# A two-layer graph network: VectorE's transposed one-hot and its copies of x columns take a second operand from PSUM

## The reference

```
for each of two layers:
    z      = concat(x[dst], x[src], edge_attr)            # 320 per edge
    msg    = sigmoid(z @ Wf + bf) * softplus(z @ Ws + bs) # 128 per edge
    summed = segment_sum(msg, dst);  cnt = segment_sum(1, dst)
    out    = batchnorm(summed / max(cnt, 1)) + x
result = layernorm(x + out of layer 2)
```

## Time and profile before

| | |
|---|---|
| time, median of 3 runs | 2116.5 us (2115.28 to 2119.24) |
| span of the profiled execution | 2110.8 us |
| VectorE busy | 1801.2 us, 85% of the span |
| ScalarE busy | 1677.5 us, 79% |
| TensorE busy (weight loads) | 1557.2 us, 74% (1286.2 us, 61%) |
| GpSimd busy | 1515.1 us, 72% |
| mean granted TensorE clock | 0.925 of full speed |
| mean busy share of the DMA engines, most of the span | about 0.53 |

### The profile page before, as it was taken

One profiled execution on the slowest core, in us unless ns is written; L12 is line 12 of the kernel. 1 busy time (PEld: TensorE's weight loads), 2 busy tenths in 40 slices (PEclk: granted clock), 3 DMA queues, 4 the chain that ended last, 5 costly groups with the idle time before them and its releaser, 6 DMA issues. The chain is left out here.

```text
span 2110.8 us, 35689 instructions
## 1 busy us (share of the span) xinstructions
PE 1557.2 (74%) x8321; PEld 1286.2 (61%) x8321; DVE 1801.2 (85%) x4354; ACT 1677.5 (79%) x2908; POOL 1515.1 (72%) x1589
## 2 busy tenths in 40 slices
PE   7777767767767787677487777777676776877773
PEld 6666656656556666566376666666565665665652
DVE  6899989989889898898549999898898887988887
ACT  5798888878878788788467888888787887887884
POOL 6677777777777777777267777777777777777770
PEclk9999999999999899999799999999999998999995
DMA  8455555555555555555475555555555555555542
GB/s 291 138 156 166 156 166 155 163 158 156 158 160 156 155 156 165 152 157 155 147 224 156 154 166 165 156 163 156 156 158 161 155 155 156 162 157 156 154 143 62
DMA packets 161806, 336.71 MB, mean 160 GB/s; under 512 B 58866, under 2 KB 85610, under 8 KB 161671
## 3 DMA queue, kind: packets, MB, share of 16 engines
q0 software_dynamic: 74496, 202.13, 32.5%
q1 hardware_dynamic: 85654, 131.58, 20.4%
q10 hardware_dynamic: 1522, 1.72, 0.3%
HBM read 315.49 MB, written 19.81 MB: 159 GB/s over the span
## 5 line engine op out<-in xcount | busy, mean ns | idle before, releaser
L344 POOL DMA_INDIRECT pre<-s_rows,ends x1512 | 1451.3, 960 | 473.8 <-issue 448.1
L458 PE MATMUL pre_ps<-rhs,lhs 128*128 128x256 f32 x3136 | 854.8, 417 | 463.5 <-DVE lhs L696 462.1
L458 PEld LDWEIGHTS pre_ps<-rhs,lhs 128*128 128x128 f32 x3136 | 607.0, 204 | 676.1 <-DVE lhs L696 385.0
L716 DVE TENSOR_TENSOR pre<-pre_ps,pre 128x1024 f32<-128x1024 f32 x378 | 460.7, 1219 | 52.6 <-DMA pre<-s_rows,ends 51.1
L548 ACT ACTIVATE pre<-pre 128x512 f32<-128x512 f32 x392 | 246.9, 630 | 309.3 <-DVE pre L716 270.0
L471 PEld LDWEIGHTS sum_ps<-hot,msg 128*128 128x128 f32 x3136 | 441.6, 204 | 53.2 <-issue 15.5
L696 DVE TENSOR_SCALAR lhs<-lhs,base_f,part 64x256 f32<-64x256 int32 x784 | 340.9, 435 | 114.2 <-issue 106.5
L471 PE MATMUL sum_ps<-hot,msg 128*128 128x64 f32 x3136 | 418.1, 279 | 24.8 <-DVE sums L736 24.8
L553 ACT ACTIVATE logs<-pre 128x1024 f32<-128x1024 f32 x392 | 414.3, 1057 | 12.4
L543 ACT COPY rhs<-dst_ps 64x256 f32<-64x256 f32 x792 | 290.0, 366 | 24.8 <-PE dst_ps L445 6.6
L727 DVE TENSOR_TENSOR msg<-soft_ps,logs 128x512 f32<-128x512 f32 x392 | 271.0, 691 | 13.6
(11 more groups left out here) (88 smaller groups left out, 570.8 us busy)
## 6 DMA issues: line engine op xcount, KB each, us to landing
lhs<-dge_and_destination_cols SPq DMA_DIRECT2D x196, 512.0 KB
pre<-s_rows,ends POOLq DMA_INDIRECT x1512
s_rows<-logs SPq DMA_DIRECT2D x8, 512.0 KB, 7.1
s_rows<-x_t SPq DMA_DIRECT2D x7, 512.0 KB, 10.8
s_rows<-msg SPq DMA_DIRECT2D x6, 512.0 KB, 6.1
x_rows<-pre SPq DMA_DIRECT2D x12, 256.0 KB, 4.5
out<-y_out SPq DMA_DIRECT2D x12, 256.0 KB, 2.3
ends<-edge_ends SPq DMA_DIRECT2D x100, 16.0 KB, 3.6
```

The lines of the kernel that those rows point to most:

```text
L344: nc.gpsimd.indirect_dma_start(pre[:, slot(k, j), i, 0:width], None, rows, bass.IndirectOffsetOnAxis(ap=ends[:, k, j * TILES + i, 0:1], ax ...
L458: ins = nc.tensor.matmul(pre_ps[:, j % 2, i, :], lhs[:, j // 2, edges], rhs[:, j, i // 2, :], start=True, stop=not plain(b, k, j))
L716: nc.vector.tensor_tensor(rows, pre_ps[:, j % 2], rows, ALU.add).then_inc(s_pre[j], 1)
```

## The change

Two groups of columns of `sum_ps` that no matmul writes get fixed contents: `part_ps` holds the partition numbers, `ones_ps` a column of ones. They are filled once a layer. The transposed one-hot becomes a `scalar_tensor_tensor` whose second tensor is `part_ps`, read with a step of zero over the 256 columns. The copies of x columns become a product with `ones_ps`. Since PE writes the same bank, VectorE's wait for the window sums of step m - 4 (`s_sum`) moves to the start of the step, both copies stand between the two additions, and PE's first window sum waits for the copies of step 3.

```diff
+        part_ps, ones_ps = sum_ps[:, 0, 0, WIN:WIN + PAIRS], sum_ps[:, 0, 1, WIN:WIN + 1]
...
             def window_sum(g, j):
                 done(pe, s_msg, g, j, 0)
                 done(pe, s_hot, g, j, 0)
+                if isinstance(g, int) and g == 0 and j == 0:
+                    pe.wait_ge(s_cols[3], 2)
                 done(pe, s_added, g, j, 1)
...
                 after(nc.vector.tensor_tensor(flag[:, 1:2], flag[:, 0:1], sum_ps[0:1, 0, 0, 0:1], ALU.add))
+                v.wait_ge(iotas, 3)
+                after(nc.vector.tensor_copy(part_ps, t["part"][:]))
+                after(nc.vector.tensor_copy(ones_ps, t["ones"][:]))
...
             else:
                 v.sem_inc(planned, 1)
+                nc.vector.tensor_copy(part_ps, t["part"][:]).then_inc(scaled, 1)
+                nc.vector.tensor_copy(ones_ps, t["ones"][:]).then_inc(scaled, 1)
+                v.wait_ge(scaled, 2)
                 v.wait_ge(cnt_in, 16)
...
-                    v.wait_ge(scaled, c + 1)
+                    v.wait_ge(scaled, c + 3)
...
-                    ins = nc.vector.tensor_scalar(lhs[hot_rows[q], j // 2, at],
-                                                  lhs[hot_rows[q], j // 2, at].bitcast(I32),
-                                                  base_f[hot_rows[q], k, PAIRS * j + q:PAIRS * j + q + 1],
-                                                  t["part"][hot_rows[q], q:q + 1], ALU.subtract, ALU.is_equal)
+                    ins = nc.vector.scalar_tensor_tensor(lhs[hot_rows[q], j // 2, at],
+                                                         lhs[hot_rows[q], j // 2, at].bitcast(I32),
+                                                         base_f[hot_rows[q], k, PAIRS * j + q:PAIRS * j + q + 1],
+                                                         part_ps[hot_rows[q], q:q + 1].to_broadcast([WIN, PAIR]),
+                                                         ALU.subtract, ALU.is_equal)
...
             def add_up(g, j, q, at):
-                done(v, s_sum, g, j, 0)
...
+            def take_window(j, q, at):
+                return nc.vector.tensor_tensor(x_cols[:, j, q, :], x[:, bass.ds(at[PAIRS * j + q], WIN)],
+                                               ones_ps.to_broadcast([P, WIN]), ALU.mult)
...
-                ins = nc.vector.tensor_copy(x_cols[:, j, q, :], x[:, bass.ds(at[PAIRS * j + q], WIN)])
+                ins = take_window(j, q, at)
...
+                if four_back:
+                    done(v, s_sum, four_back[0], four_back[2], 0)
                 if live(0):
                     hot_transposed(b, k, j)
...
                     add_up(four_back[0], four_back[2], 0, sum_at)
                 if live(0):
                     window_cols(g, j, 0, cols_at)
+                    window_cols(g, j, 1, cols_at)
                 if four_back:
                     add_up(four_back[0], four_back[2], 1, sum_at)
-                if live(0):
-                    window_cols(g, j, 1, cols_at)
```

More of the change, by code:

```diff
@@ L833, in _ @@
                 for q in range(PAIRS):
-                    ins = nc.vector.tensor_copy(x_cols[:, j, q, :], x[:, bass.ds(cols_at[PAIRS * j + q], WIN)])
+                    ins = take_window(j, q, cols_at)
                 ins.then_inc(s_cols[j], 1)
```

## The result

The changed kernel takes 2124.22 us in the median of 20 runs (2116.0 to 2129.4), the kernel before 2116.35 us (2113.49 to 2119.38, 20 runs). The ratio is 1.0035, 95% interval 1.0028 to 1.0043: 7.9 us slower, where 2104.5 us had been forecast, 12.0 less than 2116.5. The profiled execution of the changed kernel took 2124.08 us with a span of 2122.3, so 1.8 us lie around the span, not the 5.7 that the prediction took; the profiled execution of before, with 1.8 us around its 2110.8, would be shorter than each of the 20 runs.

A forecast was written before the change was run, and what follows sets the result against it. GpSimd's gathers were to bound, at 5.04 us a step. Terms -15.5 + 3.0 + 0.4 + 0.4 = -11.7 us take the 2110.8 span to 2099.1; with 5.7 around it 2104.8, rounded to 2104.5, range 2096 to 2120.

The forecast's parts named there:

- (a): GpSimd's gathers in both layers: the changed forms no longer exclude them, so they fall towards 946 ns, gaining 15.5 us.
- (b): VectorE's transposed one-hot: 479 ns as scalar_tensor_tensor instead of 435 in the mean, adding 0.09 us a step.
- (c): VectorE's copies of x columns: 222 ns without stalls, against 220 in the mean before, so the durations cancel.
- (d): VectorE's additions with both copies between them: 0.70 us instead of 0.72, and no stalls of 0.06; gain 0.08 a step.
- The sum: Steps after the change: GpSimd 5.01 us, VectorE 4.92 in layer 1; GpSimd stays the bound, leftover lag costs 1.5 a layer.
- The base: VectorE's step in layer 1 of the kernel before: 4.83 us, from 58 one-hots between 240 and 380 us.
- (e): VectorE's wait for the window sum, moved ahead of the one-hot: five late sums in 60 steps, adding 0.08 us a step.
- the second rival: Chance 0.10: the moved wait decides, turning at a VectorE step of 4.98 us; with fifteen waits in 60 steps, about 2127.
- The other two rivals: No relief for the gathers, about 2117 us, chance 0.13; operands in PSUM are dear, about 2132 us, chance 0.07.
- (f): The two fills of PSUM columns: 0.4 us more in layer 1, nothing in layer 2 under the wait for counts.
- The signs named beforehand: Among five: waits before the one-hot in tens of places, hundreds meaning the second rival; ring-slot waits over 40 us, VectorE bounds.
- The fifth sign: VectorE's waits for landed gathers shrink but don't vanish in the late part of a layer.

The follow-up runs named there:

- e17: The kernel before with only VectorE's wait for the window sum moved ahead of the transposed one-hot: 2124.95 us against 2115.8, ratio 1.0043.
- e9: The whole change, but with the second tensors of one-hot and copies in SBUF, wait still moved: 2144.76 us against 2116.61 for the kernel before, ratio 1.0125.

## Why the prediction was wrong

- *(a) GpSimd*: the mechanism was right. Expected 946 to 948 ns, measured 950 and 953, 6 to 7 ns off a gather instead of 10 to 14, so 715 x 6 + 704 x 7 = 9 us instead of 15.5. Other instructions still meet a gather; the casts are seen to. What else makes up the 4 and 7 ns by which the means exceed the median of 946 isn't shown.
- *(b) the one-hot* at 479 and *(c) the copies* at 222 ns: right (480 and 215). In the 56 steps the time from one-hot to addition, waits left out, rises from 0.92 to 1.00 us in the mean. *(d) the order*: right, 0.08 off a step (from the first addition to `sums` 0.74 us in the mean before, 0.67 after; the prediction's 0.72 without stalls adds up to 0.73).
- *VectorE's step in "The sum"*: here the prediction failed, in the sizes of two of its terms. It put the step at 4.92 us, so that VectorE would work off its 15 us by the end of layer 1 and 1.5 us a layer would be left. The step was 5.01 to 5.03 us, of the 10.4 us of lag at the 29th step 9.1 stood at the last, and the lags at the ends of the layers cost 11.0 and 3.0 us.
- *The base*, the larger of the two: 4.83 us a step, counted as 58 one-hots in one window of 140 us, where one more or less is 0.08 us a step. Over two whole bodies with their two stalls it is 4.89. With this alone, and the moved wait as forecast, the step is 4.98, the very point from which the prediction said that it turns.
- *(e) the moved wait*: "five such in 60 steps" at 0.9 us made 0.08 us a step. In the same 56 steps of layer 1 the changed kernel waits 7.8 us in six places, the kernel before 2.0 in four, so 0.10 more; over 140 steps it is 22.3 us in 17 places, 1.3 us each, 0.16 a step against 0.04 before, so 0.12 more. In e17, where nothing else changed, the wait is 0.20 a step.
- *Where the late sums were in the kernel before*: read step by step from its timeline, 15 sums in layer 1's 140 steps end after the one-hot has started, and 12 of them are among its waits; in layer 2's 29th to 168th step there are 24, and 14 are among them. A sum that ends after the one-hot's start but before the addition's was late for nobody, so the list of waits hides three in layer 1 and ten in layer 2. The changed kernel waits in 17 and 24 places: the number could have been read beforehand. The length could not: 1.3 us each in layer 1, where those of before end 1.05 us late in the mean.
- *The two together*: with 0.06 of base and 0.04 of wait VectorE's 4.92 becomes 5.02, where 5.03 was measured, beside GpSimd's 5.02. It went nearest to the second rival, which had 0.10 and the right turning point (4.98). But that rival put all of it on the wait and let layer 2 gain 6 us; here more than half of the shift came from the base, which no rival doubted, and layer 2 gained nothing. The other two rivals fall: the gathers did become shorter, and a one-hot with an operand in PSUM takes 480 ns, beside 484 with both in SBUF (medians, after and e9).
- *(f) and the turn*: in layer 1 the first one-hot starts 0.5 us later (32.6 against 32.1), as forecast. In layer 2 the fills take 0.16 and 0.15 us and lie under the wait for the counts, as forecast. Layer 2's first one-hot starts 1.1 us later than the lag explains: the wait for the DMA of the inverses is longer (6.7 us instead of 4.9), the one for the counts shorter (4.8 instead of 7.5). e17 has its lag without the fills. The 4.0 us of layer 2's first steps stand in no term of the prediction, which charged the first seven steps of layer 1 alone.
- *The signs named beforehand*: the waits before the one-hot over the whole span,

```profile
DVE lhs L705 <- PE sum_ps L474: 38.7, 31, 1.4
DVE lhs L705 <- PE sum_ps L479: 28.4, 21, 2.3
```

  52 in all, were in the tens and not in the hundreds, which was to speak for the forecast. It doesn't tell the two apart: with the little slack that there was, tens of 1.3 us are enough. GpSimd's waits for ring slots at 54.4 us, over 40, were to say that VectorE had become the bound. Its slack was used up, but the sign was right by luck: the 54.4 us are 144 pauses, of which 0.305 each, 44 us, is the pause that stands before every gather, so GpSimd was hardly held up more than before. Both kinds together are 488.3 us against 483.7 before. The fifth sign, waits for landed gathers that shrink but don't vanish, failed: none is left.

What stays open: whether the shorter gathers are worth anything at 2116 us once the wait is out of the way, and what the dearer one-hot costs there without it; the changed forms with the old wait and the one-hot made ahead never ran at 2116 us. No kernel of the runs was shown to beat the one before there.

## What to carry to other kernels

Where two engines take nearly the same time per step, the lag of the start is part of the time as soon as the second has no slack left to work it off: compare the steps over whole loop bodies, with their stalls, since one instruction more or less in a short window was worth 0.08 us a step here, more than a third of the slack. Before moving a wait to an earlier place, measure from the timeline how long after that new place the awaited thing ends, step by step and in every stage; the list of waits holds only what was late for the old place (12 of 15 in layer 1 here, 14 of 24 in layer 2). A gain on the bounding engine is worth at most the distance to the next one.

## What the runs showed of the hardware

Two tensors in SBUF hold up an indirect DMA's issue on GpSimd as a one-tensor form does, or more: 977 ns a gather in layer 2 with both second operands in SBUF (e9), 960 with the old forms, 953 with the operands in PSUM. The Trainium skill says this of an instruction with two SBUF inputs against GpSimd's reads (SBUF — State Buffer, "Who interferes with whom"); it infers there too that a two-input instruction takes only the read side of the shared ports, while writing DMA descriptors needs the write side. For the issue of a gather the runs decide otherwise, by 24 ns in layer 2 and 10 in layer 1.

And one program, the kernel before, took 2116 us on some chips, at a mean granted clock of 0.92, and 2845 to 2851 on others, at 0.76. The changed kernel and the moved wait alone are slower still on those others, at 0.80 to 0.81, so the clock alone doesn't tell the time; the traces taken there have VectorE waits of 0.5 to 0.7 ms that no recorded instruction ends.
